# A pipelined graph layer on TensorE: x also loaded transposed, the input norm folded away, logits in column tiles

## The reference

```python
def _layernorm(x, axis=-1, eps=1e-05):
    m = jnp.mean(x, axis=axis, keepdims=True)
    v = jnp.var(x, axis=axis, keepdims=True)
    return (x - m) / jnp.sqrt(v + eps)
...
    def _L0_gnn_ref(x, adj, W_t, b_t, W_h, theta):
...
        in_degrees = jnp.sum(adj, axis=-1)
        norm = jnp.power(in_degrees + 1e-06, -0.5)[..., None]
        f_hom = jnp.einsum('bnd,de->bne', x, theta) * norm
        f_hom = jnp.einsum('bnm,bmd->bnd', adj, f_hom) * norm
        f_het = jnp.einsum('bnd,de->bne', x, W_h)
        gate = jax.nn.sigmoid(jnp.einsum('bnd,de->bne', x, W_t) + b_t)
        out = gate * f_hom + (1.0 - gate) * f_het
        return jax.nn.elu(out)
...
    def _L0_ffn_ref(x, Wr, W1s, b1s, W2s, b2s, W1p, b1p, W2p, b2p):
...
        shared = gelu(x @ W1s + b1s) @ W2s + b2s
        rw = jax.nn.softmax(x @ Wr, axis=-1)
        topw, topi = jax.lax.top_k(rw, K)
```

## Time and profile before

| | us |
|---|---|
| runs shown, median | 1471.88 |
| runs shown, from and to | 1471.05 to 1473.44 |
| span of the profiled execution | 1465.8 |
| PE busy in it | 1368.2 (93%) |
| DVE, ACT, POOL busy | 968.2, 790.4, 578.6 |
| turns 1 to 7 of the front's loop begin at | 54.86 to 225.72 |

### The profile page before, as it was taken

How to read it: one execution, slowest core, us unless ns; L and a number is a source line. 1 busy time by engine, 2 the same in 40 slices (tenths; PEclk the granted TensorE clock), 3 DMA queues, 4 the chain that set the end, 5 groups by cost and what they waited for, 6 DMA issues and landing times. The chain is left out here.

```text
span 1465.8 us, 27395 instructions
## 1 busy us (share of the span) xinstructions
PE 1368.2 (93%) x10158; PEld 820.5 (56%) x10158; DVE 968.2 (66%) x2134; ACT 790.4 (54%) x1311; POOL 578.6 (39%) x502
## 2 busy tenths in 40 slices
PE   4999999887999999996899999999999789999998
PEld 2455555656999999963233333333332467764498
DVE  2467877332333333346889999999996799957633
ACT  3475655622444444434676777777774568863110
POOL 2127776651555555510121132121133599961000
PEclk9999999988999999999999999999999999999999
DMA  9857747326787777674444344333331321004034
GB/s 298 283 185 282 268 125 229 109 71 175 226 235 231 228 233 231 185 199 135 130 125 143 106 140 131 95 108 117 103 102 51 112 60 45 15 1 95 1 101 132
DMA packets 202360, 213.99 MB, mean 146 GB/s; under 512 B 22661, under 2 KB 159237, under 8 KB 202228
## 3 DMA queue, kind: packets, MB, share of 16 engines
q1 hardware_dynamic: 193588, 194.40, 43.9%
q0 software_dynamic: 8640, 17.84, 3.4%
HBM read 168.61 MB, written 43.58 MB: 145 GB/s over the span
## 5 line engine op out<-in xcount | busy, mean ns | idle before, releaser
L1493 ACT ACTIVATE c_AH<-c_S 128x2048 f32<-128x2048 f32 x128 | 240.7, 1881 | 130.0 <-PE c_S L1358 129.7
L1527 DVE TENSOR_TENSOR c_AH<-c_AH,c_A 128x2048 f32<-128x2048 f32 x128 | 292.0, 2285 | 24.5 <-ACT c_AH L1493 16.6
L841 ACT ACTIVATE a_A<-a_DG,a_A 128x256 f32<-128x256 f32 (+1 forms) x194 | 95.1, 529 | 220.4 <-PE a_DG L703 205.9
L596 POOL DMA_INDIRECT ys<-a_A,a_targets x142 | 138.4, 975 | 155.7 <-DVE a_A L1031 133.8
L571 POOL DMA_INDIRECT rows<-a_S,a_slots x128 | 132.5, 1035 | 71.7 <-issue 64.7
L1316 POOL TENSOR_TENSOR c_raw<-c_deg,c_power 128x16 f32<-128x16 f32 x16 | 58.2, 3638 | 243.0 <-DVE c_deg L1584 243.0
L1385 PE MATMUL c_DG<-c_AH,c_ones 128*32 128x512 f32 x1024 | 137.2, 608 | 8.7 <-DVE c_AH L1527 8.7
L1358 PE MATMUL c_S<-c_Q,c_K 32*128 32x512 f32 x928 | 132.3, 640 | 5.1 <-ACT c_AH L1493 3.1
L1371 PE MATMUL c_YA<-c_AH,c_XT 128*32 128x512 f32 x1024 | 131.9, 593 | 0.3 <-DVE c_XT L1594 0.3
L673 PE MATMUL a_AG<-a_A,x 128*128 128x512 f32 x256 | 114.4, 595 | 0.1
L703 PE MATMUL a_DG<-a_A 128*128 128x256 f32 (+1 forms) x340 | 102.4, 423 | 6.6 <-ACT a_A L841 4.2
(11 more groups left out here) (401 smaller groups left out, 2509.1 us busy)
## 6 DMA issues: line engine op xcount, KB each, us to landing
a_A<-in_dram SPq DMA_DIRECT2D x72, 578.0 KB
a_A<-in_dram SPq DMA_DIRECT2D x32, 1024.0 KB
c_A<-in_dram SPq DMA_DIRECT2D x128, 256.0 KB, 2.6
a_A<-rows SPq DMA_DIRECT2D x71, 130.0 KB
G<-ys SPq DMA_DIRECT2D x10, 512.0 KB, 5.1
a_X<-in_dram SPq DMA_DIRECT2D x8, 512.0 KB
a_R<-in_dram SPq DMA_DIRECT2D x8, 512.0 KB, 4.6
stream<-a_R SPq DMA_DIRECT2D x8, 512.0 KB
```

The lines of the kernel that those rows point to most:

```text
L596: pool.indirect_dma_start(ys, bass.IndirectOffsetOnAxis(ap=targets[g % NY][:, t:t + 1], axis=0), Y[g % NY][:, t, :], None, bounds_check=ys ...
L841: act.activation(hT[g % 2][:, f, 0:size(g)], up_bank(g, f)[:, 0:size(g)], ACT.Gelu, bias=w_of(g)[:, F_N + f:F_N + f + 1]).then_inc(h_ready, 1)
L1493: act.activation(AH[g % UNITS][:, :, :], S[:, :, :], ACT.Sigmoid, scale=HD ** -0.5).then_inc(att_ready, 1)
L1527: dve.tensor_tensor(ah[:, :, :], ah[:, :, :], A[g % ADJ_BUFS][:, :].unsqueeze(1).to_broadcast([P, HEADS, HALF]), ALU.mult).then_inc(ah_dve, 1)
```

## The change

The host also passes x transposed, and `load_xT` puts it where the transform reads its stationary operand, so PE transposes nothing of x. The mean is taken out by weights that one matmul centres (`centre_weights`, I - 1/128), and the factor 1/std is applied where DVE and ACT read the transform. `normalise_in`, `x_transposes` and `copy_xnT` are gone. The residual is taken from `X`, which has four buffers now and is loaded once. At the start the transform of graph 0 stands ahead of its degrees, and the degree norm is applied afterwards (`scale_first`). The logits of 1024 nodes come from four matmuls of 32 x 256 with the router's weights stationary, each in its own column group; ACT copies them (`copy_logits`) and two transposes (`logit_transposes`) put them where `choose` reads. The elu's `min` on DVE becomes a Relu ahead of the Exp on ACT. After the loop `rank` stands one `up` or `down` later.

```diff
...
-        X = [sb(f"X{u}", [P, T, D]) for u in range(2)]
-        R = [sb(f"R{u}", [P, T, D]) for u in range(2)]
+        X = [sb(f"X{u}", [P, T, D]) for u in range(4)]
         A = [sb(f"A{u}", [P, T * N]) for u in range(3)]
-        xn = sb("xn", [P, T, D])
+        XT = [sb("XT", [P, N]), xnT]
...
-            sp.dma_start(X[0][:, :, :], tiled(x_in[0])).then_inc(x_loaded[0], 16)
-
             def load_x(i):
-                wait(sp, xn_ready, i - 1)
-                sp.dma_start(X[i % 2][:, :, :], tiled(x_in[i])).then_inc(x_loaded[i % 2], 16)
+                if i >= 4:
+                    sp.wait_ge(mid_stored, 16 * (i - 3))
+                    sp.wait_ge(s_ready, 2 * (i - 3))
+                sp.dma_start(X[i % 4][:, :, :], tiled(x_in[i])).then_inc(x_loaded[i % 2], 16)
+
+            def load_xT(i):
+                if i >= 2:
+                    sp.wait_ge(fgh_psum, T * (i - 1))
+                sp.dma_start(XT[i % 2][:, :], xT_in[i]).then_inc(xT_loaded[i % 2], 16)
...
-            load_adj(0)
             for k, w in enumerate((theta, W_h, W_t)):
                 sp.dma_start(W[:, k, :], w).then_inc(w_loaded, 16)
             sp.dma_start(bias[:, :], b_t.rearrange("(a n) -> a n", a=1).to_broadcast([P, D])).then_inc(w_loaded, 16)
-            sp.dma_start(Wg[:, :], Wr).then_inc(w_loaded, 16)
+            sp.wait_ge(consts, 1)
+            sp.dma_start(Wg[:, 0:E_N], Wr).then_inc(w_loaded, 16)
+            load_x(0)
+            load_xT(0)
+            load_adj(0)
             load_x(1)
+            load_xT(1)
             load_adj(1)
-            sp.wait_ge(consts, 13)
+            sp.wait_ge(consts, 16)
             for e in range(E_N):
                 sp.dma_start(tiled(rows[E_N * CAP + e * G:E_N * CAP + (e + 1) * G, :]), no_rows).then_inc(filled, 16)
             for i in range(B):
                 if i + 2 < B:
                     load_adj(i + 2)
-                    load_x(i + 2)
                 if i >= 2:
                     store_mid(i - 2)
-                load_r(i)
+                if i + 2 < B:
+                    load_xT(i + 2)
+                    load_x(i + 2)
...
             norm_power(0)
+            n1.power(pool, power, 1, 1)
...
+                    pool.wait_ge(H_ready, T * (i + 1))
                     n1.power(pool, power, i + 2, i % 2)
...
-            def x_transposes(i):
-                pe.wait_ge(xn_ready, i + 1)
-                pe.wait_ge(deg_ready, i + 1)
-                for mm in transposes(pe, TP, xn, ident):
-                    mm.then_inc(xnT_psum, 1)
+            def centre_weights():
+                pe.wait_ge(w_loaded, 80)
+                pe.matmul(AG[:, 0:3 * D], dpart[:, 0:P], W[:, :, :].rearrange("p a n -> p (a n)"),
+                          start=True, stop=True).then_inc(Wc_psum, 1)
...
-                pe.wait_ge(xnT_ready, NH * min(i + 2, B))
+                pe.wait_ge(deg_ready, min(i + 2, B))
...
+                if i > 0:
+                    pe.wait_ge(dpart_ready, NH * i + NH)
+                else:
+                    pe.wait_ge(Wc_ready, 1)
+                pe.wait_ge(xT_loaded[i % 2], 16 * (i // 2 + 1))
                 for t in range(T):
-                    if t < NH:
-                        pe.wait_ge(xnT_ready, NH * i + NH)
-                    elif t < 4:
-                        if i >= 2:
-                            pe.wait_ge(x2T_ready, NH * (i - 2) + t - 1)
-                    else:
+                    if t >= 4:
                         pe.wait_ge(H_ready, T * i + t - 3)
-                    pe.matmul(bank(t)[:, 0:3 * D], xnT[:, t * P:(t + 1) * P],
+                    elif t >= NH and i >= 2:
+                        pe.wait_ge(x2T_ready, NH * (i - 2) + t - 1)
+                    pe.matmul(bank(t)[:, 0:3 * D], XT[i % 2][:, t * P:(t + 1) * P],
                               W[:, :, :].rearrange("p a n -> p (a n)"), start=True, stop=True).then_inc(fgh_psum, 1)
...
             def logits(r):
                 pe.wait_ge(x2T_ready, NH * r + NH)
                 pe.wait_ge(H_ready, T * min(r + 3, B))
-                for t in range(T):
-                    mm = pe.matmul(LG[:, t, :], x2T_of(r)[:, t * P:(t + 1) * P], Wg[:, :], start=True, stop=True)
+                for c in range(4):
+                    mm = pe.matmul(LT[32 * c:32 * c + 32, :], Wg[:, :], x2T_of(r)[:, bass.ts(c, N // 4)], start=True, stop=True)
+                mm.then_inc(Lt_psum, 1)
+
+            def logit_transposes(r):
+                pe.wait_ge(Lt_ready, r + 1)
+                for q in range(2):
+                    mm = pe.transpose(LG[:, q * P:(q + 1) * P], Lt[:, q * P:(q + 1) * P], ident[:, :])
                 mm.then_inc(logits_psum, 1)
...
+            def first_degrees():
+                pe.wait_ge(H_ready, T)
+                for t in range(T):
+                    if t == 0:
+                        pe.wait_ge(first_adj[0], 48)
+                    elif t == 6:
+                        pe.wait_ge(first_adj[1], 16)
+                    g = 32 * (t % 4)
+                    for h in range(NH):
+                        mm = pe.matmul(DG[g:g + 32, half(h)], ones[:, 0:32], adj(0)[:, t, half(h)], start=(t < 4), stop=(t >= 4))
+                        if t == T - 1:
+                            mm.then_inc(dpart_psum, 1)
...
-            pe.wait_ge(consts, 2)
-            degrees(0)
-            degree_transposes(0)
-            pe.wait_ge(w_loaded, 80)
-            pe.wait_ge(consts, 13)
+            pe.wait_ge(consts, 5)
+            centre_weights()
             for i in range(B):
-                x_transposes(i)
                 if i >= 2:
                     x2_transposes(i - 2)
                 if i >= 1:
                     out_transposes(i - 1)
                 transform(i)
+                if i == 0:
+                    first_degrees()
+                    degree_transposes(0)
+                    pe.wait_ge(consts, 16)
                 aggregate(i, 0)
                 if i >= 2:
                     logits(i - 2)
                 if i + 1 < B:
                     degrees(i + 1)
-                aggregate(i, 1, range(4))
+                aggregate(i, 1, range(2))
+                if i >= 2:
+                    logit_transposes(i - 2)
+                aggregate(i, 1, range(2, 4))
                 if i + 1 < B:
                     degree_transposes(i + 1)
                 aggregate(i, 1, range(4, T))
...
             logits(B - 2)
             down(0)
+            logit_transposes(B - 2)
+            up(2)
             rank(B - 2)
-            up(2)
             down(1)
             up(3)
             down(2)
             x2_transposes(B - 1)
             for g in range(4, GROUPS):
+                if g == 5:
+                    logit_transposes(B - 1)
+                if g == 6:
+                    rank(B - 1)
                 up(g)
                 if g == 4:
                     logits(B - 1)
-                if g == 5:
-                    rank(B - 1)
...
+            def copy_weights():
+                act.wait_ge(Wc_psum, 1)
+                act.activation(W[:, :, :].rearrange("p a n -> p (a n)"), AG[:, 0:3 * D], ACT.Copy).then_inc(Wc_ready, 1)
+
+            def copy_logits(r):
+                act.wait_ge(Lt_psum, r + 1)
+                act.activation(Lt[:, :], LT, ACT.Copy).then_inc(Lt_ready, 1)
...
-                    act.wait_ge(FZ_ready, T * i + t + 1)
-                    act.activation(Hh[i % 2][:, t, :], bank(t)[:, D:2 * D], ACT.Copy).then_inc(H_ready, 1)
+                    act.wait_ge(FZ_ready, T * (i + (i > 0)) + t + 1)
+                    act.activation(Hh[i % 2][:, t, :], bank(t)[:, D:2 * D], ACT.Copy,
+                                   scale=n1.rstd[i % 2][:, t:t + 1]).then_inc(H_ready, 1)
...
             def elu_exp(i):
-                act.wait_ge(O_min, i + 1)
-                act.activation(E[:, :, :], E[:, :, :], ACT.Exp).then_inc(E_ready, 1)
+                act.wait_ge(O_ready, i + 1)
+                act.activation(E[:, :, :], O[:, :, :], ACT.Relu, scale=-1.0).then_inc(below_zero, 1)
+                act.wait_ge(below_zero, i + 1)
+                act.activation(E[:, :, :], E[:, :, :], ACT.Exp, scale=-1.0).then_inc(E_ready, 1)
...
-            normalise_in(0)
-            copy_dpart(0)
+            copy_weights()
             for i in range(B):
-                copy_xnT(i)
                 if i >= 2:
                     copy_x2T(i - 2)
                 copy_H(i)
-                if i + 1 < B:
-                    normalise_in(i + 1)
+                if i == 0:
+                    copy_dpart(0)
                 if i >= 1:
                     elu_exp(i - 1)
                 copy_agg(i, 0)
+                if i >= 2:
+                    copy_logits(i - 2)
...
+            copy_logits(B - 2)
             elu_exp(B - 1)
             gelu(2)
             share(B - 2)
...
             normalise_mid(B - 1, 0)
             copy_x2T(B - 1)
             gelu(4)
+            copy_logits(B - 1)
```

(44 more changed lines are left out.)

121 lines of the change are left out of this document (57 added, 64 removed).

## The result

The changed kernel takes 1501.93 us in the median (1496.99 to 1504.5, four runs) against 1472.66 for the kernel before on the same chip: a ratio of 1.0203, with a 95% interval from 1.0184 to 1.0222. The prediction was 1472 with a range to 1482; it was wrong.

| stretch (first transform matmul, or last transposes of `carry`, to the next mark) | before | after | forecast of the difference |
|---|---|---|---|
| start to the transform of turn 2 | 81.69 | 86.77 | +3.5 |
| turns 2 to 6 | 144.03 | 155.15 | +8.6 (4.3 the chain, 4.3 the clock) |
| turn 7 to the last transposes of `carry` | 21.64 | 22.08 | 0 |
| from there to the first row transposes | 103.70 | 122.43 | -12 |
| the rest | 1114.7 | 1114.6 | 0 |

What follows compares the result with a forecast made beforehand. A loop turn was taken to cost the longer of PE's own work and the chain from `choose` to `carry`. The terms 3.5 + 4.3 + 4.3 - 12 = +0.1 gave 1472.0 us, with a range from 1455 to 1482.

Steps and rivals of the forecast that it cites:

- the chain: Loop: `choose`, `normalise_mid`, `copy_agg`, transposes of `carry`; later logits make a turn 29.7 us, +4.3 over five turns.
- the clock: Loop: PE waits about 2.9 us before `carry` each turn; half of five clock drops taken, +4.3, between 0 and 14.
- Start: Before turn 2: X(2) lands at 56.2 behind three more loads, delaying PE and lowering its clock; +3.5, from -1 to +6.
- Turns 2 to 6: Loop: `choose` begins 18.2 us after the transform's start, not 16.09; a turn of 29.7, +4.3, from -6 to +7.
- 27.5 to 27.9: Loop turn without the logits' detour: 27.5 as the term's low end, 27.9 the top of the shorter-loop rival, chance 0.24.
- 26.4 for PE alone: Loop: the us a turn would take if PE's work alone set it, after losing x's transposes and most of the logits.
- After the loop: From the last `carry` transposes to the row transposes: graph 7 scattered earlier by the new orders; -12, between -9 and -17.
- if PE waits no more than once: After the loop: condition for PE reaching `rank(7)` after 47 us instead of 62.4.
- 16.7 earlier: After the loop: scatter(7) starts at 50.2 us behind the last `carry` transposes instead of 66.9.
- late by nothing that the rows name: After the loop: unexplained late DVE and ACT releases; if repeated, 5.8 us lost, about 2 more if `gelu(2)` is late.
- the rivals: Four other outcomes: shorter loop, 0.24; clock drops each turn, 0.20; column groups don't overlap, 0.06; nothing measurable, 0.08.
- the clock in each turn: Loop rival: PE's wait ahead of `carry`'s transposes drops the clock in all five turns, 8.5 to 13.5, 1476 to 1481; chance 0.20.

Runs made afterwards that it cites:

- e4_start: Changed kernel with DVE's statistics of graph 2 moved from ahead of `read_transform(1)` to behind it: 1492.40 us, ratio 1.0130 to the kernel before.
- e3_early_logits: Changed kernel with two tiles of the aggregate's second half and the logits' two transposes moved ahead of `degrees`: 1484.93 us, ratio 1.0082 to the kernel before.
- pauses: POOL waits for landing after every fourth scatter of graphs 5 to 7: changed kernel 1482.23 us, kernel before 1465.72; graphs 5 and 6 only, kernel before 1460.17.
- eights: Changed kernel with POOL pausing after every eighth scatter behind the loop instead of every fourth: 1486.48 us, ratio 1.0100 to the kernel before.
- e6_old_tail: Changed kernel with the orders of `rank` and `share` behind the loop put back as in the kernel before: 1498.85 us, ratio 1.0196 to the kernel before.

## Why the prediction was wrong

**Start.** Right in its mechanism: DVE waits for X(2) and PE behind it; 56.85 against 56.2. The term was +3.5, the rows gave +5.1; PE waited 5.65 and not some 10, and lost 2.6 to the low clock (2.3 forecast). `e4_start` shows the cause: with the statistics behind `read_transform(1)` the aggregate begins 9.4 earlier.

**Turns 2 to 6.** Right, and nearly in size: 29.76 a turn against 29.7, 18.4 against 18.2 for `choose`. `e3_early_logits` shows that the logits' place alone makes it: 27.95, close to the figure that the prediction gave for a chain without copies and without the detour (27.5 to 27.9). There PE waits for `carry` no more, but still 0.98 in each turn for DVE ahead of the transposes of the routed rows, a wait that the forecast's 26.4 for PE alone left out.

**The clock.** The forecast took half of five drops, 4.3; four of five came, 5.5 us, within the 0 to 14. Half was a guess between none and all, so that it came near is in part luck. That PE's wait is broken up by eight transposes (0.99, then 2.03) didn't save it, though 1.88 alone had left the clock up. The rule of the Trainium skill (TensorE: Matmul & The Clock Gate, section "HAM oscillation — how this bites in real kernels") is that a loop in which PE waits long enough between its bursts of matmuls starts each burst at the lower clock. Four turns here agree; the one at 210, with waits as long (0.98 and 2.01), doesn't. `e3_early_logits`, without that wait, has no drop.

**After the loop: the step that failed.** The prediction had PE reach `rank(7)` 47 us behind the last `carry` transposes "if PE waits no more than once", and so graph 7's scatters start at 50.2, 16.7 earlier. A stretch of releases "late by nothing that the rows name" lay on that path, and it was priced at most at the 7.7 us that it had cost before. It took a delay with an unknown cause for a constant. PE reached `rank(7)` at 78.7 and the scatters started at 82.9 (346.93), 16 later than before. The releases were late not in that place alone but where POOL scattered for long without a break; PE waited 5.87, 16.91 and 12.80 for them.

That the delay belongs to the run of scatters is shown: it goes with pauses, in both kernels, is in between with eights, and moves with the run. Why the change made it worse is in part in the timelines: five scatters of graph 4 and twelve of graph 5, 0.9 apart before, became one run of 17, and graph 5's last four joined the sixteen of graph 6. `place(6)` didn't come earlier; the logits' transposes behind `down(0)` and the first late release held up `choose(6)`, and with it those four. `e6_old_tail` leaves the run of 17 and the transposes behind `down(0)` as they are, so it doesn't separate them. For graph 7 the run is the same in both kernels, and PE's wait ends 3.0 us after its last scatter before and 3.4 with the change; PE came to it 5.2 and 9.4 us ahead of that scatter's end, and this is most of the difference between 8.15 and 12.80. Why PE comes to it earlier in the run stays open.

The 16.7 were also credited to the wrong cause. With the pauses `place(7)` comes at 50.0 in the old orders: the time that the new orders were to save had been lost to late releases.

Of the rivals, the clock in each turn came nearest. None had the late releases growing, though the number to suspect stood in the text.

## What to carry over

A delay that the profile can't name is not a constant to be carried through a sum: ask first what ran beside it each time, and give it a range that lets it grow. On a program whose GpSimd issues long runs of indirect DMAs, look at releases marked "remote" and far behind the producer's end, and try a short break after every few DMAs where another engine waits for PE. A shortened stage is worth only what its chain lets through: here both engines lost work, the turn grew, and moving two transposes ahead of `degrees` made it shorter than before (27.95 against 28.54).
